# Decoder layer with a routed feed-forward: router's products taken from the sums before the last normalisation, second store buffer, new order of work

## The reference, cut to what matters

```
x = layernorm(x + attention(x, W_qkv, W_out))               # segments of 128, every second key
x = layernorm(x + cross_attention(x, ctx, Wq.., Wo, bo))    # call this x2
logits = x2 @ router_w                                      # 14 columns
e = argmax(logits);  gate = softmax(logits)[e]
x = layernorm(x2 + gate * (gelu(x2 @ w1[e] + b1[e]) @ w2[e] + b2[e]))
```

## Time and profile before

| | |
|---|---|
| median of 3 runs | 620.52 us (619.97 to 623.33) |
| the profiled execution | 628.13 us, of which its span 626.4 us |
| PE busy | 579.0 us, 92% of the span |
| DVE busy | 463.6 us, 74% |
| POOL busy | 407.6 us, 65% |
| ACT busy | 347.8 us, 56% |
| DMA, mean over the span | 80 GB/s |

### The profile page before, as it was taken

One profiled execution on the slowest core, in us unless ns is written; L12 is line 12 of the kernel. 1 busy time (PEld: TensorE's weight loads), 2 busy tenths in 40 slices (PEclk: granted clock), 3 DMA queues, 4 the chain that ended last, 5 costly groups with the idle time before them and its releaser, 6 DMA issues.

```text
span 626.4 us, 16708 instructions
## 1 busy us (share of the span) xinstructions
PE 579.0 (92%) x5652; PEld 478.2 (76%) x5652; DVE 463.6 (74%) x1067; ACT 347.8 (56%) x842; POOL 407.6 (65%) x554
## 2 busy tenths in 40 slices
PE   6989999999999999899999999866969999999990
PEld 5667778777778778678777777645859999999990
DVE  2679988998899899699898899932535666556662
ACT  1456666666575676465765766534525555555540
POOL 4365675577578577377677767762666777777762
PEclk9899999999999999899999999897979999999996
DMA  8110132144325425515415114532044433333210
GB/s 232 57 23 23 28 101 56 41 115 84 76 53 136 77 59 139 65 37 173 57 46 175 25 42 148 150 94 52 11 64 98 111 86 85 97 86 97 60 40 0
DMA packets 76419, 50.10 MB, mean 80 GB/s; under 512 B 38950, under 2 KB 70698, under 8 KB 76336
## 3 DMA queue, kind: packets, MB, share of 16 engines
q1 hardware_dynamic: 70992, 40.60, 26.8%
q0 software_dynamic: 5344, 8.44, 5.2%
HBM read 40.54 MB, written 10.60 MB: 82 GB/s over the span
## 4 chain that ended last, share of the span: by engine, by line
PE 74%; SPq 6%; DMA 5%; issue 4%; DVE 4%; POOL 3%; ACT 2%; another core or an unknown queue 0%; DVEq 0%; POOLq 0%; ACTq 0%
PE ps_r L811 21%; PE ps_r L728 12%; PE ps_r L947 11%; PE ps_s L934 10%; PE ps_r L795 4%; PE ps_s L750 4%; PE ps_s L741 3%; SPq L619 3%; PE ps_r L856 3%; PE ps_r L783 2%; PE ps_r L874 2%; DMA xres<-in_x 2%; POOL out L1551 1%; DMA xg<-x_rows,slots 1%; DVE mx L1113 1%
## 5 line engine op out<-in xcount | busy, mean ns | idle before, releaser
L1445 POOL TENSOR_TENSOR prob<-prob,rden 128x616 f32<-128x616 f32 (+1 forms) x96 | 138.5, 1447 | 84.7 <-DVE rden L1145 82.3
L1113 DVE TENSOR_REDUCE mx<-ps_s 128x8 f32<-128x616 f32 (+1 forms) x96 | 89.5, 933 | 29.8 <-PE ps_s L741 17.6
L974 ACT COPY probT<-ps_r 128x512 f32<-128x512 f32 x192 | 86.4, 480 | 45.0 <-PE ps_r L728 39.8
L1133 DVE TENSOR_REDUCE den<-prob 128x8 f32<-128x616 f32 (+1 forms) x96 | 87.9, 916 | 14.3 <-ACT prob L994 13.2
L994 ACT ACTIVATE prob<-prob 128x616 f32<-128x616 f32 (+1 forms) x96 | 79.4, 834 | 25.2 <-DVE prob L1124 24.2
L1124 DVE TENSOR_TENSOR prob<-ps_s,mx 128x616 f32<-128x616 f32 (+1 forms) x96 | 89.3, 930 | 2.2 <-PE ps_r L728 0.8
L947 PE MATMUL ps_r<-w2s,hT 128*128 x360 | 89.0, 392 | 1.3 <-issue 0.7
L728 PE MATMUL ps_r<-ident,prob 128*128 128x128 f32 (+1 forms) x576 | 88.4, 282 | 1.7 <-DVE bo_s L1257 1.1
L934 PEld LDWEIGHTS ps_s<-xgT,w1b 128*128 128x128 f32 x720 | 87.4, 192 | 2.5 <-issue 0.2
L934 PE MATMUL ps_s<-xgT,w1b 128*128 128x128 f32 x720 | 88.0, 275 | 0.0
L728 PEld LDWEIGHTS ps_r<-ident,prob 128*128 128x128 f32 (+1 forms) x576 | 64.8, 142 | 17.4 <-issue 12.0
(11 more groups left out here) (148 smaller groups left out, 1021.2 us busy)
## 6 DMA issues: line engine op xcount, KB each, us to landing
w1s<-in_w SPq DMA_DIRECT2D x14, 512.0 KB
w2s<-in_w SPq DMA_DIRECT2D x14, 512.0 KB
b2r<-in_b SPq DMA_DIRECT2D x45, 128.0 KB, 3.2
xT<-in_x_cols SPq DMA_DIRECT2D x16, 256.0 KB, 3.7
xres<-in_x SPq DMA_DIRECT2D x16, 256.0 KB
x_rows<-x2s SPq DMA_DIRECT2D x32, 128.0 KB, 2.1
xkT<-in_xk_cols SPq DMA_DIRECT2D x16, 128.0 KB, 2.8
ctxT<-in_ctx_cols SPq DMA_DIRECT2D x16, 77.0 KB
```

What stands on the lines that cost most here:

```text
L974: nc.scalar.copy(probT[0:rows, par, first:last], src[0:rows, 0:last - first]).then_inc(pT_copied[kind].sem, 1)
L1113: nc.vector.tensor_reduce(m, s, axis=AX, op=ALU.max).then_inc(max_done[kind].sem, 1)
L1133: nc.vector.tensor_reduce(den[:, par, 0:heads], prob[:, n % 3, 0:heads * width].rearrange("p (h k) -> p h k", k=width), axis=AX, op=ALU.ad ...
L1445: nc.gpsimd.tensor_tensor(p, p, rden[:, par, 0:heads, None].to_broadcast([P, heads, width]), ALU.mult).then_inc(scaled[kind].sem, 1)
```

## The change

The transposes of the normalised rows (`x2T`) and the router step (`rt`) are gone. wo becomes 272 columns wide: 16 columns behind it hold wo times the router, whose columns have lost their mean. After the two products of `ox` with 272 columns, two more with 16 columns add x1 times the router in the same bank, so `x1T` gets a second buffer and is kept until then. The residual `x1r` carries the constant part. The sums are 272 wide, and ACT makes the logits from the last columns with rstd as scale (`act_logits`), once for each half of a batch. At the start three new steps `wr` and a longer `bo` make the extra columns, from one more small load, `bo_c`. `x2s` has two buffers by batch, the ring of output rows `yo` shrinks from six to four, `logits` has two buffers. The expert's number for `y` is read behind `hid`. All orders are new; those that matter here are in the diff.

```diff
+    RC = 16
+    DR = D + RC
...
-        logits = alloc(top, "logits", [P, TPP, E])
+        logits = alloc(top, "logits", [P, 2, TPP, E])
...
-        XR = 6
+        XR, YR = 6, 4
...
-            router_s = sb1("router_s", [P, KC, RW])
-            wo_s = sb1("wo_s", [P, KC, D])
+            router_s = sb1("router_s", [P, KC, RC])
+            wo_s = sb1("wo_s", [P, KC, DR])
...
+            bo_c = sb1("bo_c", [P, KC])
...
+            x1r = sb1("x1r", [P, TPB, DR])
+            x1T = sb1("x1T", [P, 2, KC, S])
...
-            x2s = sb1("x2s", [P, TPB, D])
-            x2T = sb1("x2T", [P, KC, S])
-        fill = x2T[:].rearrange("p c s -> p (c s)")
+            x2s = sb1("x2s", [P, 2, TPB, D])
...
-            attend5:14 scores5:15 probT20:15 ox1:14 spr0:0 probT21:15 probT30:15 probT31:15 probT40:15
-            probT41:15 attend2:15 attend3:15 attend4:15 ox0:15 rows:0 probT50:15 probT51:15 hid:0 attend5:15
-            rows:1 x2T0:14 ox1:15 rows:2 rt0:14 hid:1 x2T0:15 y:0 rows:3 rt0:15 rk0:13 y:1 hid:2 tot0:1 hid:3
-            rows:4 y:2 rk0:15 spr0:1
...
+            x1T0:15 attend3:14 qx0:15 ox0:14 scores2:15 probT40:14 probT41:14 probT50:14 probT51:14 scores3:15
+            scores4:15 attend4:14 attend5:14 scores5:15 spr0:0 probT20:15 probT21:15 probT30:15 attend2:15
+            ox1:14 probT31:15 probT40:15 attend3:15 probT41:15 probT50:15 probT51:15 ox0:15 attend4:15
+            attend5:15 rows:0 rk0:13 hid:0 rows:1 ox1:15 hid:1 y:0 rows:2 rows:3 y:1 hid:2 tot0:1 rk0:15 rows:4
+            hid:3 y:2 spr0:1
...
+            r_max0:15 r_is_max0:15 r_weigh0:15 bias:0 ln20:15 res:0 r_first0:15 stat:0 prepare2:0 ln21:15
+            r_onehot0:15 agg:0 prepare3:0 prepare4:0 eps:0 bias:1 r_gate0:13 plan0:1 plan1:1 r_pick0:15 res:1
...
-            gather:0 scale5:15 gather:1 gather:2 r_less_max0:13 rstd21:14 gather:3 rstd20:15 rstd21:15 gather:4
-            r_count0:13 r_count_tile1:13 r_count_tile2:13 gather:5 r_count_tile3:13 gather:6 r_count0:15
-            r_less_max0:15 r_count_tile1:15 r_count_tile2:15 r_count_tile3:15 pow:0 enter0:13 enter0:15
...
+            scale2:15 r_count0:13 scale3:15 r_count_tile1:13 rstd20:14 r_less_max0:13 r_count_tile2:13
+            r_count_tile3:13 scale4:15 scale5:15 gather:0 x1r0:15 gather:1 rstd21:14 gather:2 gather:3
+            r_count0:15 rstd20:15 rstd21:15 gather:4 gather:5 gather:6 r_less_max0:15 r_count_tile1:15
+            r_count_tile2:15 r_count_tile3:15 pow:0 enter0:13 enter0:15
...
-            place_v4@2 load_e0@5 load_ctx0@-2 load_xres0@0 load_x0@-2 place_v0@1 place_v1@1 place_v2@1
-            place_v3@1 store_x0@3 place_v4@1 store_x1@3 load_xres0@-1 store_x0@2 place_v0@0 place_v1@0
-            load_x0@-3 place_v2@0 store_x1@2 place_v3@0 load_e0@4
...
+            load_xres0@2 load_x0@1 load_e0@3 load_e0@2 store_x0@6 place_v0@3 place_v1@3 place_v2@3 place_v3@3
+            place_v4@3 store_x1@6 load_ctx0@0 place_v0@2 load_x0@0 place_v1@2 place_v2@2 store_x0@5 store_x1@5
+            load_xres0@1 place_v3@2 place_v4@2
...
-        PE_TILES = "rows@-1 y@1 hid@-1"
-        ACT_TILES = "gelu@0 wa@-2 rows@-2"
-        DVE_TILES = "res@2 stat@2 norm@3 wd@-3 agg@2 eps@2 bias@1"
-        POOL_TILES = "pow@3 gather@-4 put@4"
-        SP_TILES = "slots@-3 bias_row@4"
+        PE_TILES = "y@2 hid@0 rows@-1"
+        ACT_TILES = "wa@-2 rows@-2 gelu@-1"
+        DVE_TILES = "eps@1 bias@0 wd@-4 res@0 stat@0 norm@1 agg@0"
+        POOL_TILES = "gather@-3 pow@3 put@4"
+        SP_TILES = "slots@-2 bias_row@-2"
...
+                with nc.allow_non_contiguous_dma("a bias by partitions"):
+                    load("small", bo_c[:], bo.rearrange("(c p) -> p c", p=P))
...
+            if job == "wr":
+                if k == 0:
+                    last = project(lambda c: ones[:], lambda c: router_s[:, c, :], width=RC)
+                elif k == 1:
+                    for h in range(KC):
+                        for c in range(KC):
+                            last = transpose(dst[:, h * D + c * P:h * D + (c + 1) * P], wo_s[:, c, h * P:(h + 1) * P])
+                else:
+                    pe.wait_ge(taken["wr"].sem, taken["wr"].at(0, 1))
+                    for h in range(KC):
+                        last = project(lambda c: woT[:, c, h * P:(h + 1) * P], lambda c: router_s[:, c, :],
+                                       dst[:, h * RC:], RC)
+            elif job == "bo":
+                pe.wait_ge(taken["wr"].sem, taken["wr"].at(0, 2))
                 for c in range(KC):
-                    last = nc.tensor.matmul(dst[:, 0:D], bv_s[:, c:c + 1].to_broadcast([P, P]), wo_s[:, c, :],
-                                            start=(c == 0), stop=(c == KC - 1))
+                    nc.tensor.matmul(dst[:, 0:DR], bv_s[:, c:c + 1].to_broadcast([P, P]), wo_s[:, c, :],
+                                     start=(c == 0), stop=False)
+                for c in range(KC):
+                    last = nc.tensor.matmul(dst[:, D:DR], bo_c[:, c:c + 1].to_broadcast([P, P]), router_s[:, c, :],
+                                            start=False, stop=(c == KC - 1))
...
-            elif job == "x2T":
-                for t in range(TPB):
-                    wait(pe, ln_done[2], b, t, held="pe_job.2", part=t)
-                    for c in range(KC):
-                        last = transpose(dst[:, c * S + t * P:c * S + (t + 1) * P], x2s[:, t, c * P:(c + 1) * P])
...
-                last = project(lambda c: oTx[:, c, cols], lambda c: wo_s[:, c, :])
-            elif job == "rt":
-                wait(pe, taken["x2T"], b, held="pe_job.11", part=part)
-                for t in range(TPB):
-                    last = project(lambda c: x2T[:, c, t * P:(t + 1) * P], lambda c: router_s[:, c, :],
-                                   dst[:, t * RW:], RW)
+                for c in range(KC):
+                    nc.tensor.matmul(dst[:, 0:DR], oTx[:, c, cols], wo_s[:, c, :], start=(c == 0), stop=False)
+                for c in range(KC):
+                    last = nc.tensor.matmul(dst[:, D:DR], x1T[:, b % 2, c, cols], router_s[:, c, :],
+                                            start=False, stop=(c == KC - 1))
...
+            wait_plan(pe, j)
+            expert[j] = expert_of(pe, j)
...
-            elif job == "x2T":
-                wait(act, computed["rt"], b - 1, held="act_take.9", part=job)
-                if b == 0:
-                    act.wait_ge(lists_filled.sem, lists_filled.at(0))
-                last = nc.scalar.copy(x2T[:].rearrange("p c n -> p (c n)"), src)
-            elif job == "rt":
-                wait(act, routed["less_max"], b // 2 - 1, held="act_take.10", part=job)
-                wait(act, routed["is_max"], b // 2 - 1, held="act_take.11", part=job)
-                last = nc.scalar.copy(logits[:, b % 2 * TPB:(b % 2 + 1) * TPB], src[:, 0:TPB * RW].rearrange("p (t e) -> p t e", t=TPB)[:, :, 0:E])
...
+        def act_logits(act, t, b):
+            wait(act, routed["less_max"], b // 2 - 2, held="act_logits.1", part=t)
+            wait(act, routed["is_max"], b // 2 - 2, held="act_logits.2", part=t)
+            wait(act, rstd_done[2], b, t, held="act_logits.3", part=t)
+            nc.scalar.activation(logits[:, b // 2 % 2, b % 2 * TPB + t], sums(2, t)[:, D:D + E], ACT.Copy,
+                                 scale=rstd[:, 2 + t:3 + t]).then_inc(logits_made.sem, 1)
...
-                wait(dve, computed["x2T"], b - 1, held="dve_layernorm.4", part=2 * which + k)
-                wait(dve, x2_stored[k], b - 1, held="dve_layernorm.5", part=2 * which + k)
-                dst = x2s
-            nc.vector.tensor_scalar(dst[:, k, :], sums(which, k)[:], mv[:, q, 0:1], rstd[:, q:q + 1],
+                wait(dve, x2_stored[b % 2][k], b // 2 - 1, held="dve_layernorm.5", part=2 * which + k)
+                dst = x2s[:, b % 2]
+            nc.vector.tensor_scalar(dst[:, k, :], sums(which, k)[:, 0:D], mv[:, q, 0:1], rstd[:, q:q + 1],
...
+            src = bank_of("bo", "0", 0)
+            nc.vector.tensor_tensor(bo_s[:], src[:, 0:D], bo_s[:], ALU.add)
+            nc.vector.tensor_copy(x1r[:, :, D:], src[:, None, D:DR].to_broadcast([P, TPB, RC])).then_inc(bo_ready.sem, 1)
+        def dve_router(dve, k):
+            src = bank_of("wr", str(k), 0)
+            wait(dve, computed["wr"], 0, k, held="dve_router.1", part=k)
+            if k == 0:
+                dve.wait_ge(w_loaded["small"].sem, w_loaded["small"].at(0))
+                last = nc.vector.scalar_tensor_tensor(router_s[:], src[:, None, 0:RC].to_broadcast([P, KC, RC]), -1.0 / D,
+                                                      router_s[:], ALU.mult, ALU.add)
+            elif k == 1:
+                last = nc.vector.tensor_copy(woT, src[:, 0:KC * D].rearrange("p (c d) -> p c d", c=KC))
+            else:
+                last = nc.vector.tensor_copy(wo_s[:, :, D:], src[:, 0:KC * RC].rearrange("p (c e) -> p c e", c=KC))
+            last.then_inc(taken["wr"].sem, 1)
```

(26 more changed lines are left out.)

268 lines of the change are left out of this document (137 added, 131 removed).

## The result

The changed kernel takes 594.8 us (median of 4 runs, 593.6 to 596.2) where the kernel before, on the same chip, takes 621.7 (619.97 to 623.33): ratio 0.957, 95% interval 0.953 to 0.961, 26.9 us less. The forecast was 603, range 595 to 613: right in sign, 8 us too high, and the result lies 0.2 us outside the range.

The account below looks back on a forecast made before the run. PE was taken as the bound, with DVE 10% below, plus how soon tile 7 starts. Terms 5.5 - 1.0 + 15 = 19.5 us, less 2, from the 620.5 median gave 603 us, range 595 to 613.

Parts of the forecast that it names:

- Handover: Between attention and tile stages, last scores to tile 7's transposes: 15 us gained, bounds 3 and 19.
- The first leg: Last scores to ox1:15: 18.2 us falls to 13.2, 5.0 less.
- The second: From ox1:15 to POOL's first list write: 21.5 us falls to 9.3, 12.2 less.
- The third: From POOL's first list write to tile 7's landed rows: 19.7 us, no change.
- Steady part: Attention stage, batches 0 to 13: PE saves 0.39 us net per batch, 5.5 us in all.
- Start: Before steady batches: extra PE and DVE work partly fills a wait; a loss of 1.0 us, bounds +1 and -4.
- The 2 us taken off for the profiled execution: Whole kernel: gain cut by 2 us because the removed stalls may partly be the profiled run's excess over the median.
- SP, tiles and end: Transfers, tile stage and finish: PE stays the bound at the same rate; 0, bounds 0 and -1 us.
- Rivals: Waits move 17% (613 us), slower 5% (627), no change 4% (620), all gone 3% (596), narrow products nearly free 2% (590).
- No wait of PE for `vX`: Attention periods: late V pieces would make PE wait every period, 24 us lost, 627 us; chance 5%.
- the logits' scalings waited for no rstd: ACT in attention batches: waiting priced at 0, bounds 0 to 0.5 us per batch; such waiting would show the forecast wrong.
- tile 7 still waits: End of handover: PE still waits about 5 us; alternative, rows come before PE, a further 7 us, 596, chance 3%.

Follow-up runs that it names:

- before_again: The kernel before, unchanged, profiled a second time on another, slower chip: 646.9 us in one execution.
- after_again: The changed kernel, unaltered, run once more on a second chip: 594.3 us, ratio 0.957 to the kernel before there.
- before_two_stores: The kernel before with a second x2s store buffer, four yo rows and ys moved in memory, old router step and order: 639.5 us, ratio 0.985 to the kernel before.
- old_order: The changed kernel with all engines' lists put back to those of the kernel before, new steps placed in them: 658.1 us, ratio 1.014 to the kernel before.
- apart: The changed kernel with four entries of TensorE's list moved so steps of one kind stand apart: 602.7 us, ratio 0.970 to the kernel before.
- joined: The changed kernel with four pairs of probability transposes put side by side in TensorE's list: 601.2 us, ratio 0.970 to the kernel before.

## Why the prediction was right or wrong

- **Handover, 15 us: right, with some luck in the legs.** 14.5 measured, and 12.5 between before_again and after_again. The first leg gained 1.9 and not 5.0: its steps ran at a granted clock of 0.74 and I had summed them at the full one, and PE waits 0.6 us for one of ACT's copies. The second gained 10.2 where 12.2 were expected. The third gained 2.3 where nothing was: the gather is issued 11.6 us behind the first write (11.3 before), but its rows are there after 5.9 us instead of 8.5 (424.55 to 430.40; 455.31 to 463.76). That is scatter of single executions: the same gather took 6.3 us in before_again, 6.1 in before_two_stores and 6.8 in after_again, and the leg 18.8, 18.5 and 18.3. old_order (11.1 us from the last `kx` to the end) and before_two_stores (8.5) show that most of the gain can be had with the old order, and 8.5 from the buffer alone.
- **Steady part, 5.5 us: the step that failed.** It was 10.2 for eleven batches at the rate of the clean periods, where the forecast has 4.3 for eleven: 1.86 us a period, not 0.78. The instructions explain some 0.45 of the missing 1.08. The removed transposes cost 1.12 with their joints (1.00 expected), the narrow products 1.68 us for four steps (1.88 expected, what the router's cost before), the wider `ox` 0.08 (0.22 expected). The other 0.6 is the list's order, a term that the prediction doesn't have: I took PE "busy" for PE "at its fastest". By the sum of the steps it went at steps that both kernels have (value steps -0.27, `wout` products -0.20, x1T's -0.19, x1's transposes -0.19, `ctxT` products -0.14, the q and k products -0.18, with +0.45 for the `vx` products and +0.09 for the ranks the other way). apart (+0.95), joined (+0.85) and old_order (+0.8 on before) show that an order moves a period by as much as the whole computed gain of 0.78. All three were longer, in part by joints and in part by waits for DVE and ACT. With the old order the priced gain did not come at all.
- **Start, -1.0 us: +1.15 up to the first key product in these two profiles, but the sign is not shown.** The new products do fill the wait, 2.59 to 1.57 us. Up to the first product (6.58 us, 7.65 before) there is 1.07 of the gain, and the same kernel before reaches it at 6.72 us in before_again. Here before_again and then after, with the clock of the window from 15 us:

```profile
6.72 1.89 PE L811 MATMUL ps_r<-xT,wqkv_s 128*128 128x256 f32 x8
...
28.81 1.32 PE L811 MATMUL ps_r<-ctxT,wT 128*128 128x154 f32 x8
...
15.00:20.00 5.00, 5.00 (x32) 3.78 (x26) 4.48 (x5) 2.12 (x4) 1.76 (x3) 0.66 0.11 36
```

```profile
6.58 1.97 PE L822 MATMUL ps_r<-xT,wqkv_s 128*128 128x256 f32 x8 [0.19 <-issue]
...
29.63 1.22 PE L822 MATMUL ps_r<-ctxT,wT 128*128 128x154 f32 x8
...
15.00:20.00 5.00, 5.00 (x33) 4.44 (x27) 4.52 (x6) 2.28 (x4) 1.67 (x3) 0.66 1.04 361
```

  From the first product to the first `kx` before took 23.13 us with clocks of 0.50 and 0.87 from 15 to 25 us, before_again and before_two_stores 22.09 with 0.66 and 1.00, after and after_again 23.04 with 0.66 and 1.00. At equal clocks the change costs 0.95 us there, as forecast. The clock is worth as much: joined, which has the start of after, took 21.75 us with 1.00 in both windows. The next 0.7 of the 1.9 belongs to the steady work of batches 0 and 1 (42.75 and 42.06 us from `kx` to `kx`). The load of `bo_c` made nobody wait: 3.5 us to land, `bv_s` 3.3 beside it. The Trainium skill's rule on non-contiguous pieces ("DMA: Bandwidth & Descriptors", "Rules for kernel authors") holds in the count, 272 more packets on the queue, 256 of which would be `bo_c`; at this size they cost nothing that the trace shows.
- **The 2 us taken off for the profiled execution: wrong as a reason.** What the profile of before had more were mostly its three long periods, and I had counted no change there in any case. The other parts, 1.9 + 10.2 + 14.5 + 0.8 = 27.4 us, are near the measured 26.9. That fit is partly luck: 1.1 of the start and some 2 of the third leg are scatter, and the earlier clean periods gained more than 1.86.
- **SP, tiles and end, 0:** right, 0.8.
- **Rivals.** None came. No wait of PE for `vX` appeared in any period of after, the logits' scalings waited for no rstd (DVE waited for them twice, 2.5 us in all), and tile 7 still waits (4.10 us).

1.9 - (-1.0), 10.2 - 5.5, 14.5 - 15, 0.8 and the 2 off make 9.9 us more than forecast, and the medians 9.4. The largest of these is the steady part. The range was too narrow because that term was bounded by instruction prices alone; the order's part had no bound.

## What to carry to other kernels

Where an engine is without gaps, price a step by the change of the whole period when it goes, not by its instructions: joints between kinds of work and the place in the list count, and so does the next engine: where DVE is only 5 to 10% below, a step taken from PE can leave a wait of nearly its own length (0.73 for 0.94 us). A change of computation and the order that suits it are one edit; with the old order it gave no shorter period. Compare starts and single transfers in more than one profile before giving them a sign. Of several edits that remove one wait, count the wait once.

## What the runs showed of the hardware

- An fp32 product step with 16 columns costs nearly what one with 64 does: 16 instructions in 1.68 us against 1.88. What the two share is the 128x128 weights of each instruction (a load has a mean of 195 and 196 ns); that the load sets the time was not tested. 272 columns instead of 256 cost 0.01 us an instruction or less.
- Two value steps on TensorE cost 0.14 us more apart than together (1.16 against 1.02), and a lone set of four transposes 0.05 to 0.18 beyond its 0.44.
- The start of one kernel is not the same in each execution: TensorE's first product of before came at 7.65 and at 6.72 us, and the clock from 15 to 20 us was 0.50 and 0.66.
- The same indirect gather of 128 rows took 5.4 to 8.5 us from issue to TensorE's use of the rows, in twelve profiles in which TensorE waited for it.
- ScalarE can stop 1.3 to 3.8 us in front of a ready instruction with no releaser in the profile, on one chip twice in most periods at the same place of the program, with the clock down behind it (0.86 and 0.71). The cause is open. It was not tried.
